# A GRU and an attention GRU on one core: bodies of 64 steps on three engines, and one product in two column halves

## The reference

```
z = sigmoid(x Wxz + h Whz + b);  r = sigmoid(x Wxr + h Whr + b)
hh = relu(x Wxh + b + r * (h Whh + b));  h = z * h + (1 - z) * hh
```

```
r = sigmoid(x Wxr + h Whr + b);  c = relu(x Wxc + b + r * (h Whc))
h = (1 - a) * h + a * c
```

## Time and profile before

| | us |
|---|---|
| median of 3 runs | 4424.12 (4422.9 to 4429.71) |
| the profiled execution | 4430.53 |
| its span in the trace | 4428.7 |

### The profile page before, as it was taken

How to read it: one execution, slowest core, us unless ns; L and a number is a source line. 1 busy time by engine, 2 the same in 40 slices (tenths; PEclk the granted TensorE clock), 3 DMA queues, 4 the chain that set the end, 5 groups by cost and what they waited for, 6 DMA issues and landing times.

```text
span 4428.7 us, 336421 instructions
## 1 busy us (share of the span) xinstructions
PE 4372.4 (99%) x131196; PEld 3968.0 (90%) x131196; DVE 4196.2 (95%) x24625; ACT 2286.8 (52%) x9363; POOL 2717.1 (61%) x6154
## 2 busy tenths in 40 slices
PE   8999999999999999999998999999999999999999
PEld 7888888888888888888887999999999999999998
DVE  8999999999999999999998999999999999999999
ACT  5666666666666666666654444444444444444444
POOL 6777777777777777777773444444444444444444
PEclk9999999999999999999998999999999999999999
DMA  3333333333333333334334555555555555554554
GB/s 110 115 116 123 115 116 123 115 115 121 117 115 120 119 115 120 119 115 121 118 123 129 129 132 128 128 132 128 128 133 128 128 133 128 128 133 129 127 133 115
DMA packets 169275, 544.13 MB, mean 123 GB/s; under 512 B 31644, under 2 KB 38060, under 8 KB 169260
## 3 DMA queue, kind: packets, MB, share of 16 engines
q1 hardware_dynamic: 169260, 543.93, 44.3%
HBM read 405.24 MB, written 138.56 MB: 123 GB/s over the span
## 4 chain that ended last, share of the span: by engine, by line
DVE 52%; PE 21%; issue 20%; DMA 3%; DVEq 2%; SPq 1%; ACT 0%; ACTq 0%; PEldq 0%
DVE vec_bank L525 12%; DVE gated L448 8%; DVE state L538 7%; DVE a_new L532 6%; DVE vec_bank L455 5%; DVE gated L519 5%; DVE vec_bank L464 5%; DVE h L475 4%; PE r_bank_a L561 4%; PE r_bank_b L561 3%; DMA logits<-logit_rows 2%; PE logit_bank L623 2%; PE z_bank_b L569 2%; PE z_bank_a L569 2%; PE c_bank_a L561 1%
## 5 line engine op out<-in xcount | busy, mean ns | idle before, releaser
L331 POOL TENSOR_TENSOR a_kept<-attn_rest,state 128x128 f32<-128x128 f32 x2048 | 933.6, 456 | 1173.6 <-DVE state L538 1139.0
L314 POOL TENSOR_TENSOR kept<-z_gate,h 128x128 f32<-128x128 f32 x2048 | 933.6, 456 | 533.8 <-ACT z_gate L360 512.0
L304 POOL TENSOR_TENSOR prod<-h,qw 128x128 f32<-128x128 f32 x2050 | 934.6, 456 | 0.0
L569 PE MATMUL r_bank_a<-x,weights 64*64 64x128 f32 x8200 | 881.7, 290 | 12.8 <-ACT r_gate L389 7.1
L569 PE MATMUL r_bank_b<-x,weights 64*64 64x128 f32 x8192 | 892.8, 295 | 0.0
L569 PE MATMUL z_bank_a<-x,weights 64*64 64x128 f32 x8200 | 853.9, 283 | 0.0
L569 PE MATMUL z_bank_b<-x,weights 64*64 64x128 f32 x8192 | 843.3, 283 | 0.0
L623 PE MATMUL logit_bank<-prod,row_sum 64*64 64x128 f32 x8208 | 798.5, 270 | 8.6 <-ACT logit_rows L349 5.0
L464 DVE SCALAR_TENSOR_TENSOR vec_bank<-vec_bank,z_rest 128x64 f32<-128x64 f32 x4096 | 735.9, 225 | 0.4 <-issue 0.3
L475 DVE TENSOR_TENSOR h<-vec_bank,kept 128x64 f32<-128x64 f32 x4096 | 721.3, 218 | 0.0
L389 ACT ACTIVATE r_gate<-r_bank_a 128x128 f32<-128x128 f32 x1024 | 284.0, 277 | 837.5 <-PE r_bank_a L561 837.5
(11 more groups left out here) (119 smaller groups left out, 17857.4 us busy)
## 6 DMA issues: line engine op xcount, KB each, us to landing
x<-in_keys_t SPq DMA_DIRECT2D x512, 256.0 KB, 3.7
gru_outputs<-h SPq DMA_DIRECT2D x256, 512.0 KB, 2.9
x<-gru_outputs SPq DMA_DIRECT2D x512, 256.0 KB, 3.7
attn<-attention SPq DMA_DIRECT2D x512, 256.0 KB, 3.9
logits<-logit_rows SPq DMA_DIRECT2D x258, 8.0 KB
time_rows<-logits SPq DMA_DIRECT2D x2, 896.0 KB, 7.0
attention<-time_rows SPq DMA_DIRECT2D x2, 896.0 KB, 5.5
weights<-in_weight_columns SPq DMA_DIRECT2D x2, 176.0 KB, 3.7
```

The source lines that it names most:

```text
L304: nc.gpsimd.tensor_tensor(prod[:, (s - 1) % BODY, gcols(g)], h_at(s - 1)[:, gcols(g)], qw[:, gcols(g)], ALU.mult).then_inc(prod_ready[g], 1)
L314: nc.gpsimd.tensor_tensor(kept[:, g], z_gate[:, g], h_at(s - 1)[:, gcols(g)], ALU.mult).then_inc(kept_ready[g], 1)
L331: nc.gpsimd.tensor_tensor(a_kept[:, s % 2, gcols(g)], attn_rest[:, s % 2, gcols(g)], state[:, (s - 1) % 2, gcols(g)], ALU.mult).then_inc(a ...
L569: last = nc.tensor.matmul(dst[lanes(half)], weights[lanes(1 - half), w], moving[lanes(1 - half)], start=start, stop=False, skip_group_chec ...
```

## The change

- SPAN = 8 * BODY = 64. DVE, ACT and POOL write out 64 steps per body of both loops, in 16 passes. PE and SP keep bodies of 8 steps.
- Since PE takes its semaphores down every 8 steps, waits for constants go by s % BODY. `r_ready` and `ar_ready` become two semaphores each, one for even and one for odd steps, taken down by half as much. The extra waits and increments at s = 0 (`bodies_begun`) are gone.
- DVE gets two registers that are set with `count`; the next step's number is computed in the second half-step between candidate and new state, ahead of the place where it is used. The numbers for `stored` and `pairs` are computed for each 8 steps.
- In the GRU loop the first column half of h raises `h_begun` and the second `h_ready`. PE multiplies for r in two products of 64 columns, each waiting for its own half.

```diff
+SPAN = 8 * BODY
@@ gpsimd, scalar: both loops
-            with pool.Fori(0, T, BODY) as t0:
-                for s in range(BODY):
+            with pool.Fori(0, T, SPAN) as t0:
+                for s in range(SPAN):
...
-                    if s == 2:
-                        copy_logits(t0)
+                    if s % BODY == 2:
+                        copy_logits(t0 + (s - 2))
@@ vector
             def gru_gated(due, s, g):
-                if s == 0:
-                    dve.wait_ge(r_summed[g], due)
-                    dve.sem_inc(bodies_begun, 1)
                 dve.wait_ge(rh_summed[g], due)
-                dve.wait_ge(r_ready[g], s + 2)
+                dve.wait_ge(r_ready[g][s % 2], by_parity(s))
...
-                            dve.wait_ge(outs_stored[s // CHUNK], stored)
-                    last = nc.vector.tensor_tensor(h_at(s)[:, gcols(g)][:, c], new[:, c], kept[:, g, c], ALU.add)
-                last.then_inc(h_ready[g], 1)
-
-            with dve.Fori(0, T, BODY) as t0:
-                stored = t0 * ONES + 16
-                for s in range(BODY):
-                    due = t0 + (s + 2)
+                            dve.wait_ge(outs_stored[s // CHUNK % 2], stored)
+                    nc.vector.tensor_tensor(h_at(s)[:, gcols(g)][:, c], new[:, c], kept[:, g, c],
+                                            ALU.add).then_inc((h_begun, h_ready)[part][g], 1)
+
+            counts = [dve.alloc_register(f"dve_count_{i}") for i in range(2)]
+
+            def count(i, base, more):
+                dve.reg_add(counts[i % 2], base, more)
+                return counts[i % 2]
+
+            with dve.Fori(0, T, SPAN) as t0:
+                soon = count(0, t0, 2)
+                for s in range(SPAN):
+                    due = soon
+                    if s % CHUNK == 0:
+                        stored = t0 * ONES + 16 * (s // BODY + 1)
                     for g in GROUPS:
                         gru_gated(due, s, g)
                         gru_cand(due, s, g)
+                        if g == 1:
+                            soon = count(s + 1, t0, s + 3)
                         gru_new(due, s, g)
                         gru_h(due, stored, s, g)
...
             def agru_gated(due, s, g):
-                if s == 0:
-                    dve.wait_ge(ar_summed[g], due)
-                    dve.sem_inc(bodies_begun, 1)
-                dve.wait_ge(ar_ready[g], s + 2)
+                dve.wait_ge(ar_ready[g][s % 2], by_parity(s))
                 dve.wait_ge(rc_summed[g], due)
...
                     agru_cand(due, s, 1)
+                    soon = count(s + 1, t0, s + 3)
                     agru_new(due, pairs, s, 1)
@@ tensor
-                        pe.wait_ge(h_ready[g], s + 1)
-                        own(r_bank[g][:, 0:GC], GH_R, hs, False, True).then_inc(r_summed[g], 1)
-
-
-                        pe.wait_ge(r_ready[o], seen_by_pe(s, o))
+                        for part, c in PARTS:
+                            pe.wait_ge((h_begun, h_ready)[part][g], s + 1)
+                            last = own(r_bank[g][:, c], GH_R, hs[:, c], False, True)
+                        last.then_inc(r_summed[g], 1)
+
+
+                        pe.wait_ge(r_ready[o][(n - 1) % 2], by_parity(n - 1))
```

More of the change, by code:

```diff
@@ L26, in recurrent_attention_kernel @@
     BM = HALVES * COLS // P
-    assert HALVES == 2 and GC == P and T % BODY == 0
+    assert HALVES == 2 and GC == P and T % SPAN == 0
     BODIES = T // BODY
@@ L56, in part_sems, with parity_sems @@
             return [[sem(f"{name}_{'ab'[g]}{part}") for part, _ in PARTS] for g in GROUPS]
+        def parity_sems(name):
+            return [[sem(f"{name}_{'ab'[g]}_{('even', 'odd')[parity]}") for parity in range(2)] for g in GROUPS]
         weights = sb("weights", [P, 11, U])
@@ L126, in recurrent_attention_kernel, with by_parity @@
             sems(name) for name in ("axr_summed", "axc_summed", "ar_summed", "rc_summed"))
-        ar_ready, rest_ready = sems("ar_ready"), sem("rest_ready")
+        rest_ready = sem("rest_ready")
         agated_ready, acand_ready = sems("agated_ready"), sems("acand_ready")
-        anew_ready = [[sem(f"anew_ready_{'ab'[g]}{parity}") for parity in range(2)] for g in GROUPS]
+        r_ready, ar_ready, anew_ready = parity_sems("r_ready"), parity_sems("ar_ready"), parity_sems("anew_ready")
         s_ready, akept_ready = sems("s_ready"), sems("akept_ready")
         out_stored, table_loaded = sem("out_stored"), sem("table_loaded")
-        FIRST = BODY + 1
+        FIRST, HALF = BODY + 1, BODY // 2
         def seen_by_pe(s, g):
             return s + 2 if g == 0 else (s + 1 if s else FIRST)
+        def by_parity(s):
+            return s % BODY // 2 + 1
         ANEW = [s // 2 + 1 + s % 2 for s in range(BODY)]
@@ L338, in _ @@
                 act.sem_inc(zr_ready[g], FIRST)
-                for q in (r_ready[g], ar_ready[g]):
-                    act.sem_inc(q, (1, FIRST)[g])
+            act.sem_inc(r_ready[1][1], HALF)
+            act.sem_inc(ar_ready[1][1], HALF)
             act.sem_inc(rest_ready, 1)
@@ L349, in copy_logits @@
                 nc.scalar.activation(logit_rows[:], logit_bank[:, 0:COLS], ACT.Copy).then_inc(logits_copied, BODY)
-            with act.Fori(0, T, BODY) as t0:
-                for s in range(BODY):
-                    if s == 2:
-                        copy_logits(t0)
+            with act.Fori(0, T, SPAN) as t0:
+                for s in range(SPAN):
+                    if s % BODY == 2:
+                        copy_logits(t0 + (s - 2))
                     due = t0 + (s + 2)
@@ L388, in _ @@
                         act.wait_ge(ar_summed[g], due)
[L389 removed]
+                        nc.scalar.activation(r_gate[:, g], r_bank[g][:, 0:GC], ACT.Sigmoid).then_inc(ar_ready[g][s % 2], 1)
                         if g == 0:
@@ L460, in gru_new @@
                 for part, c in PARTS:
-                    dve.wait_ge(cand_ready[g][part], (due, s + 2)[part])
+                    dve.wait_ge(cand_ready[g][part], (due, s % BODY + 2)[part])
                     if part == 0:
-                        dve.wait_ge(zr_ready[g], s + 2)
+                        dve.wait_ge(zr_ready[g], s % BODY + 2)
                     nc.vector.scalar_tensor_tensor(new[:, c], cand[:, c], 0.0, z_rest[:, g, c],
@@ L539, in agru_sum @@
                                         a_kept[:, s % 2, gcols(g)], ALU.add).then_inc(s_ready[g], 1)
[L541 to L545, removed]
+            with dve.Fori(0, T, SPAN) as t0:
+                done, soon = t0 + 1, count(0, t0, 2)
+                for s in range(SPAN):
+                    due = soon
+                    if s % CHUNK == 0:
+                        pairs = t0 * PAIRS + 32 * (s // BODY + 1)
                     agru_gated(due, s, 0)
@@ L657, in _ @@
                         gru_x_r(o, n, (zr_ready[g], -BODY) if first else (h_ready[g], -BODY) if final else None,
-                                (cand_ready[g][1], -BODY) if first else None)
+                                (cand_ready[g][1], -BODY) if first else (h_begun[g], -BODY) if final else None)
                         pe.wait_ge(xz_summed[g], s + 1)
@@ L674, in _ @@
                             mm.then_inc(logits_summed, 1)
+                        elif final:
+                            mm.then_inc(prod_ready[g], -BODY)
                         pe.wait_ge(cand_ready[o][1], seen_by_pe(s, o))
-                        used = ((x_used, CHUNK) if g == 0 and s % CHUNK == CHUNK - 1
-                                else (r_ready[o], -BODY) if n % BODY == 0 else None)
-                        gru_x_h(o, n, (xr_summed[o], n + 1), used, (prod_ready[g], -BODY) if final else None,
+                        seen = (r_ready[o][(n - 1) % 2], -HALF) if (n - 1) % BODY >= BODY - 2 else None
+                        used = (x_used, CHUNK) if g == 0 and s % CHUNK == CHUNK - 1 else None
+                        gru_x_h(o, n, (xr_summed[o], n + 1), used or seen,
+                                seen if used else (prod_ready[g], -BODY) if g == 1 and final else None,
                                 (xr_summed[o], -BODY) if final else None)
```

36 lines of the change are left out of this document (19 added, 17 removed).

## The result

| | before | after |
|---|---|---|
| median, us | 4426.3 (4 runs) | 4527.26 (4524.89 to 4528.94, 4 runs) |
| ratio, 95% interval | | 1.0228 (1.021 to 1.0245) |
| span of the profiled execution | 4428.7 | 4525.2 |

The changed kernel is slower by 101 us. The forecast was slower by 22.

What follows compares the result with a forecast made beforehand. DVE was taken to bound the GRU loop. GRU terms -54 + 48 + 37 + 30 and attention terms -77 - 23 + 31 + 30 gave +22 us, 4446 us; 8-in-10 range 4335 to 4530.

Steps and rivals of the forecast that it cites:

- turns spared, GRU: GRU loop: 112 inner body boundaries lose DVE's turn, 0.48 us each, 54 us taken away.
- copy waits for its store: GRU loop: without DVE's turn ScalarE's logits copy waits for the last store's landing, 0.43 us more per boundary, 48 us given back.
- new code, GRU: GRU loop: DVE stalls 0.25 us per 128 instructions of new code at 186 places, 37 us added after overlap.
- turns that fetch, GRU: GRU loop: DVE's turns to code no longer held cost 2.0 us each, 30 us added.
- count moved, attention: Attention loop: DVE's step count moves off the gating, step of 1.89 us instead of 1.96, 77 us taken away.
- turns spared, attention: Attention loop: DVE's turn goes but PE's stays and costs 0.18 us, 0.21 us per boundary, 23 us taken away.
- new code, attention: Attention loop: DVE stalls 0.25 us per 128 instructions of new code at 123 places, 31 us added.
- turns that fetch, attention: Attention loop: DVE's turns to code no longer held cost 2.0 us each, 30 us added.
- Turns that have to fetch: Both loops: 30 turns to code no longer held at 2.0 us, taken from the small logits store, 60 us added.
- rival 4: Turns of both loops: fetching is dear, 4497 us at 3.7 us per turn, 4608 with two fetches, middle 4550; chance 0.16.
- The rivals with free crossings: Both loops: new code costs nothing; 4378 us if turns still fetch (chance 0.20), 4318 if turns are free too (0.12).
- Rival 3: Attention loop: r's gate holds the step, so the moved count is given back, 46 us worse, 4492 us; chance 0.15.

Runs made afterwards that it cites:

- experiment 5: Changed kernel with two buffers for the copied logits, so ACT's copy waits for the store of two bodies ago: 4455.83 us, 1.007.
- experiment 4: Changed kernel with SyncE's loads of x in the loops cut to 1/32 of the bytes, as many DMAs: 4464.62 us, 1.0093.
- experiment 3: Changed kernel with bodies of 64 steps on DVE alone, 8 on ACT and POOL: 4514.77 us; on ACT and POOL alone, 8 on DVE: 4377.96 us.
- experiments 2: Changed kernel with bodies of 16 steps instead of 64 on DVE, ACT and POOL: 4638.38 us, 1.0482.
- experiment 6: Halves alone on the kernel before: 4415.27 us; changed kernel, bodies of 8, one r product: 4333.81 without h_begun, 4329.18 with it raised, 4393.8 with both waits.

## Why the forecast was wrong in size

The mechanisms named were those found, and the sign with them; one term was mis-sized. Measured values are from the starts of the gating instructions, over all passes: a regular step is the median, and what a boundary, a copy or a turn costs is what its half-steps take above that. For a turn these are the half-step that holds it and the four behind it, less what a boundary cost before.

| term of the sum | forecast | measured |
|---|---|---|
| turns spared, GRU | -54 | -51: a boundary of 8 adds 0.20 us where it added 0.65 |
| copy waits for its store | +48 | +58: 0.60 us each (experiment 5), 0.08 before |
| new code, GRU | +37 | +36: nine places of 0.16 to 0.29 us in a body of 64 |
| turns that fetch, GRU | +30 | +63: 4.2 us each |
| column halves, and the count in the GRU loop | 0 | -10: a regular step of 2.146 instead of 2.156 us |
| count moved, attention | -77 | -89: 1.876 instead of 1.963 us |
| turns spared, attention | -23 | -17: a boundary adds 0.35 us where it added 0.50; PE's own turn costs 0.25 us there, not 0.18 |
| new code, attention | +31 | +28 |
| turns that fetch, attention | +30 | +77: 5.1 us each |
| sum | +22 | +95; the spans differ by 96.5 |

The step that failed is "Turns that have to fetch": 60 us against 140, that is 2.0 us per turn against 4.7. The other terms add up to -38 forecast and -45 measured, with misses of up to 12 us that happen to cancel; with 4.7 in place of 2.0 the forecast would have been 4527 us. That the sign came out right rests on this term too: without it the sum is below zero.

I took the landing of the small logits store for the length of a fetch. The stop alone takes 3.7 us in the GRU loop and 4.2 in the attention loop, from the branch to the next instruction, and 2.8 and 2.9 even where next to no x is loaded (experiment 4). It falls on the very boundary at which SyncE loads x: I had looked at the neighbours of the copy, but not at what runs on the DMA engines when DVE turns. And the turn isn't over with it. In the GRU loop the block behind the target comes late as well, 0.5 to 0.8 us; in the attention loop PE works at 1.2 GHz behind the turn, which makes up the 1.3 us that the four half-steps take over (experiment 4). The upper end that I gave, 3.7 us for a load, was near the truth for the stop alone; rival 4, with 3.7 to 7.4 us per turn, names the right mechanism, and its middle value of 4550 was nearer than the forecast.

The nearest row was a poor guide because it measured another thing: from the store's issue to its landing there is one transfer, from the branch to the next instruction there is a transfer that starts 1.6 us late and 1.6 us until the engine goes on (medians of the GRU loop, DVE alone, experiment 3).

The rivals with free crossings fell by the rows themselves: new code costs 0.24 us for every 128 instructions, as the three stalls of the first passes had it. The Trainium skill (Runtime: NRT & Kernel Launch, "Instruction fetch mechanics") says that a taken branch to a block that isn't held waits for a DMA; the trace agrees, 3.7 to 4.2 us. It says too that the crossing of a block is mostly hidden, and that blocks have 256 instructions; here the crossings cost 0.24 us and the packets hold 128.

Rival 3 fell: r's gate is ready in time for a step of 1.87 us. The copy's wait was right to a fifth, by the argument from what is late next: the turn of DVE had covered a DMA's landing.

## What to carry to other kernels

A longer loop body spares turns only as long as it is held by its engine. Here 280 instructions were and 324 were not; all counted, a held turn cost 0.5 to 0.7 us and one that fetches 4.9 to 5.6. So count the instructions of a body, waits and register operations too, before it is unrolled, and look for packets of code on the page. What a stall of the bound engine covers is late when the stall goes: look for the DMA whose landing falls into it, and give it a second buffer. And of a wait that is added ahead of an instruction on the critical way, count what the sequencer needs for it (0.1 us here), even where its semaphore has been raised before the other one.

## What the runs showed of the hardware

- DVE and ACT ran loops of up to 245 and 280 instructions without fetching; loops of 324 (POOL), 370 (DVE) and 475 (ACT) fetched at each turn (experiments 2 and 3). Code came in packets of 8192 bytes, some 128 instructions.
- A turn to code that wasn't held took 3.7 us (GRU loop) and 4.2 us (attention loop) until the next instruction, 2.8 and 2.9 without most of the loads of x beside it, with a second stop of 0.5 to 1.0 us in the GRU loop.
- PE's granted clock was 0.50 for 3.4 us (at three turns 6.8) behind 28 of the 30 turns of the changed kernel, at which PE had stood still for 2.1 to 2.7 us in the GRU loop and 3.0 to 4.1 in the attention loop. In experiment 4 it was so behind 12 of 30, after 1.2 to 1.5 and 2.3 to 2.6 us; with long bodies on ACT and POOL alone behind all 15 turns of the GRU loop, after 2.0 to 2.6 us. The pause's length alone does not tell the cases apart.
- With the clock at 0.50 behind a turn of the attention loop the four half-steps took 5.3 us, with the clock at 1.00 they took 3.84 (experiment 4).
- With a second semaphore wait ahead of it PE's product started 0.15 us behind h instead of 0.05, and the kernel took 61 us more (experiment 6).
